# One core's transformer block: who issues half of the key loads in the first stage

## What is computed

```python
h = layernorm(x) * (1 + ca) + sa          # ca, sa, ga, ... from silu(c) @ w_mod
q, k, v = split(h @ W_attn)               # 16 heads of 16 channels
att = softmax(causal(q @ k.T / 4)) * decay_weight_matrix(T)
x = x + ga * ((att @ v) @ W_proj)
h = layernorm(x) * (1 + cb) + sb
x = x + gb * (h @ (W + up_aux @ lora_up @ lora_down @ down_aux).T + b)
```

## Time and profile before

| | us |
|---|---|
| median of 3 runs | 1539.15 |
| lowest, highest | 1534.87, 1539.32 |
| the profiled execution's own time | 1538.15 |
| its span, first to last instruction | 1535.4 |
| busy: PE, ACT, DVE, POOL | 1266.4, 1297.5, 1000.6, 203.1 |
| mean granted clock of TensorE | 0.964 |

### The profile page before, as it was taken

One profiled execution on the slowest core, in us unless ns is written; L12 is line 12 of the kernel. 1 busy time (PEld: TensorE's weight loads), 2 busy tenths in 40 slices (PEclk: granted clock), 3 DMA queues, 4 the chain that ended last, 5 costly groups with the idle time before them and its releaser, 6 DMA issues.

```text
span 1535.4 us, 28806 instructions
## 1 busy us (share of the span) xinstructions
PE 1266.4 (82%) x11067; PEld 746.4 (49%) x11067; DVE 1000.6 (65%) x2058; ACT 1297.5 (85%) x2628; POOL 203.1 (13%) x429
## 2 busy tenths in 40 slices
PE   7875188898988898888888898989898888888774
PEld 5533044555555555555555555555555444444332
DVE  4642167777777777777777777777777666655552
ACT  3433089999999999999999999999999999999990
POOL 0322000020202011010202020202011110102022
PEclk9988589999999999999999999999999999999996
DMA  4999920000000000000000000000000000000000
GB/s 157 205 228 200 174 78 12 12 19 25 19 25 18 25 18 25 19 21 14 15 21 18 25 18 26 18 25 19 25 15 26 15 25 16 25 12 8 21 4 12
DMA packets 94448, 64.63 MB, mean 42 GB/s; under 512 B 59595, under 2 KB 89570, under 8 KB 94306
## 3 DMA queue, kind: packets, MB, share of 16 engines
q1 hardware_dynamic: 94306, 62.75, 18.0%
HBM read 41.74 MB, written 20.97 MB: 41 GB/s over the span
## 4 chain that ended last, share of the span: by engine, by line
PE 38%; DVE 26%; ACT 13%; issue 9%; POOL 1%; DMA 0%; SPq 0%; ACTq 0%; DVEq 0%
PE fast_s_ps L848 13%; DVE fast_negmax L1077 11%; PE fast_t_ps L897 10%; ACT fast_s_ps L1024 8%; DVE fast_probsT L1096 6%; PE fast_t_ps L866 5%; PE fast_t_ps L882 5%; ACT fast_probs L1024 5%; PE fast_t_ps L926 4%; DVE fast_probsT L1086 4%; DVE fast_y_sb L1115 1%; DVE fast_xb L1129 1%; DVE fast_xb L1152 1%; DVE fast_tT L1122 1%; PE fast_t_ps L908 1%
## 5 line engine op out<-in xcount | busy, mean ns | idle before, releaser
L1024 ACT ACTIVATE fast_s_ps<-fast_s_ps,fast_negmax 128x1024 f32<-128x1024 f32 (+4 forms) x768 | 786.1, 1025 | 12.3 <-PE fast_s_ps L848 11.6
L848 PE MATMUL fast_s_ps<-k_stack,fast_q_stack 96*128 96x512 bf16 (+3 forms) x2448 | 643.7, 354 | 123.4 <-ACT fast_probs L1024 83.3
L1024 ACT ACTIVATE fast_probs<-fast_s_ps,fast_negmax 128x640 f32<-128x640 f32 (+7 forms) x512 | 431.2, 842 | 66.2 <-DVE fast_negmax L1077 61.6
L1077 DVE TENSOR_REDUCE fast_negmax<-fast_s_ps 128x1 f32<-128x640 f32 (+4 forms) x512 | 397.8, 777 | 40.2 <-PE fast_s_ps L851 35.0
L1086 DVE TENSOR_TENSOR fast_probsT<-fast_t_ps,fast_dec_c 128x384 f32<-128x384 f32 (+2 forms) x512 | 276.5, 540 | 202.4 <-PE fast_t_ps L866 202.4
L848 PEld LDWEIGHTS fast_s_ps<-k_stack,fast_q_stack 96*128 96x128 bf16 x2448 | 203.1, 98 | 326.1 <-ACT fast_probs L1024 136.9
L866 PE MATMUL fast_t_ps<-ident,fast_probs 128*128 128x128 f32 x1488 | 252.4, 277 | 29.4 <-DVE fast_y_sb L1115 20.8
L1096 DVE TENSOR_TENSOR fast_probsT<-fast_t_ps,fast_dec_c 128x256 f32<-128x256 f32 x464 | 192.3, 414 | 115.0 <-PE fast_t_ps L882 115.0
L866 PEld LDWEIGHTS fast_t_ps<-ident,fast_probs 128*128 128x128 f32 x1488 | 172.3, 142 | 84.0 <-DVE fast_y_sb L1115 27.9
L882 PE MATMUL fast_t_ps<-ident,fast_probs 128*128 128x128 f32 x912 | 196.4, 296 | 20.1 <-DVE fast_tT L1122 6.4
L897 PE MATMUL fast_t_ps<-fast_probsT,fast_vals 128*16 128x128 f32 x4800 | 179.7, 275 | 23.3 <-DVE fast_probsT L1096 22.3
(11 more groups left out here) (110 smaller groups left out, 724.8 us busy)
## 6 DMA issues: line engine op xcount, KB each, us to landing
parts_d<-part SPq DMA_DIRECT2D x24, 512.0 KB, 11.5
k_stack<-parts_d SPq DMA_DIRECT2D x96, 128.0 KB, 7.4
fast_q_stack<-parts_d SPq DMA_DIRECT2D x384, 32.0 KB, 1.9
fast_vals<-v_d SPq DMA_DIRECT2D x36, 128.0 KB, 2.4
xs<-x_dram SPq DMA_DIRECT2D x8, 512.0 KB, 8.6
v_d<-w SPq DMA_DIRECT2D x8, 512.0 KB, 12.1
fast_xb<-x_dram SPq DMA_DIRECT2D x32, 128.0 KB, 2.2
out_dram<-fast_xb SPq DMA_DIRECT2D x32, 128.0 KB, 1.8
```

What stands on the lines that cost most here:

```text
L848: last = nc.tensor.matmul(s_ps[:, n % SLOTS, o:o + w], q, k_stack[:, h, P * b0 + o:P * b0 + o + w], start=True, stop=not diag)
L1024: nc.scalar.activation(dst, src, ACT.Exp, bias=negmax[:, p % 2, side, h:h + 1], scale=-1.0, accum_out=sums[:, p % 2, side, h, c:c + 1]).th ...
L1077: nc.vector.tensor_reduce(out=negmax[:, p % 2, side, h:h + 1], in_=s_ps[:, n % SLOTS, max(0, cols - P * WIN):cols], axis=AX_X, op=ALU.min) ...
```

## The change

The 12 loads of `stack_keys` are divided. A helper `stack(eng, g, js)` issues the loads of the blocks `js` on the engine's own queue. SP issues blocks 0 to 2 at the place where it issued all six. ACT issues blocks 3 to 5 of group g - 1 after its `body(g)`, that is after the cast of group g's mid part, and those of the last group at the end, each time after waiting itself for the three stores of that group. Since the calls differ by group, ACT's sequence is written out for all eight groups and no longer uses `paired`.

```diff
+            def stack(eng, g, js):
+                for j in js:
+                    for m in range(2):
+                        eng.dma_start(k_stack[HD * j:HD * (j + 1), QH * m:QH * (m + 1), g * GT:(g + 1) * GT],
+                                      parts_d[PAIRS[j][1], g, :, m, :].rearrange("(h d) t -> d h t", d=HD)
+                                      ).then_inc(k_loaded if g < NG - 1 else k_last, 16)
...
@@ sync, stack_keys
-                    for j, (_, kp) in enumerate(PAIRS):
-                        for m in range(2):
-                            sp.dma_start(k_stack[HD * j:HD * (j + 1), QH * m:QH * (m + 1), g * GT:(g + 1) * GT],
-                                         parts_d[kp, g, :, m, :].rearrange("(h d) t -> d h t", d=HD)
-                                         ).then_inc(k_loaded if g < NG - 1 else k_last, 16)
+                    stack(sp, g, range(0, 3))
...
@@ scalar
-                paired(act, NG, body)
+                def stack_keys(g):
+                    for n in range(PARTS):
+                        act.wait_ge(part_stored[n][g % 2], (g // 2 + 1) * 16)
+                    stack(act, g, range(3, len(PAIRS)))
+
+                for g in range(NG):
+                    body(g, g % 2, g // 2, min(g, 2), min(NG - 1 - g, 2))
+                    if g > 0:
+                        stack_keys(g - 1)
+                stack_keys(NG - 1)
```

## The result

| | before | changed |
|---|---|---|
| median, us | 1537.01 (4 runs, 1533.77 to 1539.32) | 1513.31 (4 runs, 1512.91 to 1513.55) |
| ratio | | 0.9843, interval 0.9821 to 0.9865 |
| span of the profiled execution | 1535.4 | 1511.0 |

The change saves 24 us, 1.6%. The page of the changed kernel has the rows of the DMA engines, which answer to the earlier trace rows, and now two queues: q1 is SP's, q10 ACT's (packets, MB, share of 16 engines).

A forecast was written before the change was run, and what follows sets the result against it. The prediction took the first stage as bound by DMA, by slow key loads to 16 partitions. Gains of 29.7 us in seven intervals and 7.3 in the tail, 37.0 from 1538.15, gave 1501.2, by the median 1502; range 1492 to 1540.

The forecast's parts named there:

- The bound: First stage: DMA engines full, paced by key loads at 119 GB/s, limited at the 16 written partitions; intervals 18.1 us.
- a pair of loads goes in the time of one: Key loads on two queues at different blocks: six loads by 1.10 us, 6.6 us a set instead of 13.2.
- The overlap with large transfers: Each interval: ACT's key loads beside SP's large transfers slow these by 1.5 us, at most 2.0, at least nothing.
- The tail: First stage's end, last key loads to PE's start: 11.1 us for 18.37, a gain of 7.3 (bounds 0 and 8.1).
- its own signs: If right: key loads 200 GB/s or more, last set near 147 us, PE's scores near 158, ACT's idle below 5.
- full overlap: Likeliest case: key loads on two queues run fully in pairs; own range 1490 to 1512 us, chance 0.50.
- (a): DMA engines serialise the two queues, intervals keep 18.1 us: 1538, or 1532 with 5% overlap; chance 0.25 with (d).
- ACT's side: ACT's rounds: wait for three stores already over, six issues of 2.8 us per group hidden in idle; cost nothing.
- Code written out: ACT's sequence, two more bodies without loop registers: costs nothing, with a microsecond on both sides.
- (d): ACT's DMAs share SP's queue after all: as (a); chance 0.25 with (a).
- (b): Half overlap: key loads on two queues at 155 GB/s, intervals 16.6 and 15.3 us, 1519 us; chance 0.17.
- (c): Slower: two queues make key loads lose rate; at 100 GB/s 2.5 us more a set, by eight, 1558; chance 0.08.

The follow-up runs named there:

- Sets 1, 4 and 9: Loads alone on one queue, 12 of 128 KB: to adjacent partitions 16.08 us, to spread partitions 9.98 us, over 128 partitions (52 ns a packet).
- the probe: No kernel computation: 17 sets of transfers run by themselves, varying queues and written partitions; 12 key loads took 16.08 us on one queue.
- heads_rotated: Changed kernel with half the heads of every block on each queue, ACT starting three blocks on, so at different blocks; 1516.63 us, ratio 0.9837.
- same_block: Changed kernel with loads divided by heads, not blocks, so both queues write to the same block when side by side; 1535.85 us, ratio 0.9960.
- all_act: Changed kernel with all 12 key loads on ACT's queue and none on SP's; 1514.11 us, ratio 0.9825.
- probe_mix: No kernel computation: one group's 12 key loads and four 512 KB stores by themselves, in six forms, each twice; one queue 20.0 us, loads on ACT 18.1.
- same_block_again: The kernel of same_block run once more, on the chip of heads_rotated; 1532.87 us, ratio 0.9941.
- set 6: In the probe: loads to block 0 alone, six times over, on one queue; 17.05 us.
- set 7: In the probe: loads to block 0 on SP's queue with block 4 on ACT's; 12.85 us.
- spread_one: Kernel before, all loads on SP, with block j in partitions j, j + 6, ... of key and query stacks; 1505.37 us, ratio 0.9780.

## Why the prediction was right, and where it was not

- *The bound* was right: the first stage hung on the DMA engines, on the rate of the key loads. Sets 1, 4 and 9 of the probe show what was argued from the earlier trace rows, that the written partitions set it and not the size of a run, its source or the number of bytes.
- *The step that failed in size* is "a pair of loads goes in the time of one", 6.6 us for a set instead of 13.2. With key loads on both queues the changed kernel moved 143 to 171 GB/s, not 238. At its 156 a set takes 10.1 us, so the step brought 3.1 us of 6.6; in the probe, where the loads stand alone, 1.9 (14.19 for 16.08). The sign of the mechanism was right (heads_rotated against same_block). My argument passed from "the limit is at the block" to "the engines are free meanwhile". The share of 1.16 in the earlier trace rows said that they are not; as I read it, an engine that holds a slow packet for one block can't serve the other queue meanwhile. No run looked at single engines.
- *The overlap with large transfers* was priced as a cost of 1.5 us. It came out as a gain: 5.2 + 10.1 are 15.3 us and the four intervals without tokens took 14.6 in the mean, 6.5 + 10.1 are 16.6 and the three with tokens took 15.6. The two errors, 3.5 us too little and some 2.3 too much, partly cancel: 15.0 us an interval for the 13.9 of the forecast. That such overlap gains is shown by all_act, with 14.7 us an interval where the bytes one after the other make 18.4 to 19.7, and by probe_mix (sets 1 and 4, 20.0 and 18.1 us).
- *The tail* should have fallen to 11.1 us and was 16.56, by the same step: key and query loads at 144 GB/s on two queues, not 238 for the keys. With spread partitions it was 14.18, with fewer issues 11.3. The lower bound by issues had 5.1 us for twelve queries, where the earlier trace rows have 6.08 and the changed kernel 5.51; it did not bind.
- *By its own signs* full overlap did not come: not 200 GB/s, the last set at 156.39 and not near 147, PE's first scores 16.6 us after it and at 172.95, not 158, and ACT's idle 5.0 to 6.2 us and not below 5. 1513 lies outside that case's own range, 1490 to 1512. It lies in the stated range because that was drawn wide, down to rival (a), where nothing is gained; it says little for the central case, which had half of the chances.
- *ACT's side* was right. Its new wait ends before the mid cast does, as forecast (83.26 and 83.88 us in the round shown); the issues take 2.7 to 3.9 us of each round, in idle time that shrank to 5.0 to 6.2 us. all_act shows what they cost once that cover is gone.
- *Code written out* costs nothing that can be measured, as taken.
- *The rivals*: (a) and (d), that the engines serialise the two, are refuted by the ratio; q10 is a queue of its own. (b), half overlap, with 155 GB/s, 16.6 and 15.3 us an interval and 1519, is nearest, on the slow side of the truth: 156 GB/s in the window shown, 15.6 and 14.6 us, and 1513. I gave it 0.17. (c) did not come. One argument against it was wrong: "no window of key loads is below 119" holds for the earlier trace rows alone, and the kernel before moved 114 GB/s from 56 to 64 us.
- *The Trainium skill.* The rule in "DMA: Bandwidth & Descriptors", Issuing engines are not separate DMA queues (only issue time is saved), does not hold here: 1.6% of the kernel was saved while SP's issues were not on the path, and heads_rotated is 16 us faster than same_block_again with the same issues on the same two engines. Its warning that all queues end on the same engines is what my step overlooked. The +6% of "SBUF — State Buffer" for two DMAs at partitions 0 and 64 compares with a rate a third higher here for blocks 0 and 4 (set 6 to set 7, 17.05 to 12.85 us, start and end included). By its table the 16 partitions of a spread block lie on 13 or 14 of the 16 ports and not on 4, which fits the gain of the step of 6; no run here looked at single ports. The prediction's "agrees" is generous, as 119 is above the 104 GB/s of the page and 155 further. And in every kernel here that has the queues at different blocks, the blocks at the same place in the two lists also lie on different ports by that table, so no run tells different blocks from different ports.

## What to carry to other kernels

When a DMA is slow, divide the engines' busy time by the packets and compare with loads of the same size to other partitions. Here it was 154 ns for 1 KB against 50, with the destination alone changed: then the larger cure is where it writes (36 us by medians for spread_one), not who issues it (24 for the change). A second queue gains something if its transfers are unlike the first's (other partitions, or large ones beside small ones) and little if they are alike (at the same block 15 to 19 of the 24 us were lost), so order the two lists apart. Count what the issues cost the engine that makes them, in its own round and at the stage's end, where nothing covers them.

## What was not expected of the hardware

- Twelve loads of 128 KB to 16 partitions with a step of 6 took 9.98 us, to 16 adjacent ones 16.08, start and end included; each cost 0.60 us to issue and not 0.43.
- By themselves, key loads on two queues took 12% less time at different blocks, and at the same block no less than the repeat of one queue. Inside the kernel that difference was 16 us of 1533.
- Key loads beside large transfers of another queue gain as much as key loads beside key loads: in probe_mix twelve loads on ACT and four stores on SP took 18.1 and 17.8 us, with the loads divided between the two queues 17.4 and 19.1, all on one queue 20.0 and 20.6.
